# The first layer norm moved into the scan, chunk by chunk, with identity products in TensorE's waits

## The chip, the core and the metric

The kernel runs on one core of a Trainium2 chip. Its time is device time in microseconds (us), from the first to the last instruction of one execution. Before the change three runs took 568.33, 569.10 and 570.53 us; the median is 569.1.

The engines are named as the profile does: PE is TensorE's matmul, PEld its weight load, DVE is VectorE, ACT ScalarE, POOL GpSimd, SP SyncE. A "q" behind the name (SPq, ACTq) is the engine's sequencer, which issues DMAs and waits.

## What is computed

Two blocks with a residual each, on `x` of shape 4 x 1024 x 128:

```python
h = _layernorm(x, axis=-1) * (1 + ca) + sa
x = x + ga * _L0_attn_ref(h, W_Q, W_KV, W1, b1, W2, b2)
h = _layernorm(x, axis=-1) * (1 + cb) + sb
x = x + gb * _L0_ffn_ref(h, ...)           # 8 experts, 2 chosen per token, and a shared one
```

The first block is a scan over the 1024 time steps. At each step the four batches' `k_t` and `v_t` (from `kv = h @ W_KV`) give one step of gradient descent on a small MLP, and the MLP as it stands at the end maps `q = h @ W_Q`:

```python
def step(params, kvt):
    k_t, v_t = kvt
    g = jax.grad(loss_fn)(params, k_t, v_t)     # loss: mean((silu(k W1 + b1) W2 + b2 - v)^2)
    return tuple((p - LR * gp for p, gp in zip(params, g))), None
params, _ = jax.lax.scan(step, (W1, b1, W2, b2), (k, v))
```

`sa`, `ca`, `ga`, `sb`, `cb`, `gb` are six rows per batch, `silu(c) @ wmod`.

## The kernel before

**Stages.** Four blocks of code follow each other. Each block has one stream of instructions per engine, and a barrier of all five engines ends it: the next block begins when the last engine, SP included, has come to the end of its stream.

1. *Prologue* (lines 188 to 408). `x` is loaded to `xr` in quarters `s_x[0..3]` (SP, 16 DMAs of 128 KB), the weights by ACT's queue. DVE takes `bn_stats` of all 32 chunks and computes mean and reciprocal root in two halves (`spread`, 16 small steps each). POOL normalises the first 12 chunks, DVE the other 20, into `hstage`; PE turns them (32 transposes); ACT applies scale and shift per batch (`modulate`) and writes `hT`, the transposed `h` of all chunks.
2. *Scan* (lines 410 to 1274). The 1024 steps are cut into 32 chunks (`CH`) of 32 steps x 4 batches = 128 columns. Within a chunk the recurrence is solved by repeated passes over 128 x 128 matrices. The steps have names: `q_...` prepare a chunk (`q_proj`: k and v from `hT`; `q_copy` to `kv`; `q_turn`, `q_rows`, `q_shift`: their transposes; `q_gram`, `q_mask`: the masked products `GX`; `q_low`: a bf16 copy `GXb`). `l_...` are the passes in bf16, `h_...` the passes in fp32 on the same chunk one turn later, `x_...` an extra pass for chunk 0, `c_...` a check of how far the last pass moved. In the names `act` is silu, `tan` its tanh, `less` is a - 1, `slope` the derivative, `tq`/`rq` a transpose and its copy back, `y` the forecast, `e` its error, `f` the error sent back, `g` the gradient, `z` the preactivation, `W1`/`W2`/`b1`/`b2` the updates.
3. *The step-by-step scan* is skipped where the check holds, as it does here.
4. *Tail* (from line 1276): `q` through the MLP, second layer norm, routing, experts, output.

**What sets the order in the scan.** `turn(n, r)` is a list written out by hand per engine: `do(step, n + k, r + k)` places the step of chunk n + k in turn n. It runs for n = -3 to 32: turns -3 to 3 straight, turns 4 to 27 in a loop of 6 x 4 turns (`Fori(1, CH // RING - 1)`), turns 28 to 32 straight. An engine works through its list in order, each step waiting for the semaphores of its inputs, so a step that waits holds up all that stand behind it on its engine.

The lines that the prediction speaks of most, all on PE in this list: `l_f1` (line 494, `bank<-W2pL,e2L`), `l_y4` (`bank<-aL,W2pL` behind `l_te`), `h_zp` (`bank<-GXb,gL` behind `l_y4`), `h_tq0` (line 607, `bank<-ident,qH`), `l_te4` (line 572). Almost all matmuls bear line 494, that of the helper `mm`.

Of the kernel before, what the change touches and what calls it, by code (L numbers as in the profile page):

```python
# [60 lines left out]
def program(nc, x, w_q, w_kv, w1, b1, w2, b2, w_router,  # L61
            s_w1t, s_b1, s_w2t, s_b2, cond, w_mod, slabs, ident_in, before_in, lower_in, tabs_in, xs, ys, out):
    with ExitStack() as ctx:
# [122 lines left out]
        POOL_NORMS = 3  # L186
        with ExitStack() as stack, block() as blk:  # L187
            psb = phase(stack)
            difq, nrq, epsq = (psb(n, [P, CH]) for n in ("difq", "nrq", "epsq"))
# [61 lines left out]
            def _(act):
# [34 lines left out]
                for g in range(NG):  # L286
                    modulate(g)
# [1931 lines left out]
```

## Time and profile before

| | |
|---|---|
| median of 3 runs | 569.1 us |
| profiled execution | 572.98 us, its span 571.2 us |
| prologue | 0 to 35.8 us |
| scan | 35.8 to about 294 us |
| tail | from 294.6 us |
| busy in the span | PE 90%, DVE 71%, ACT 65%, POOL 56% |

Times in the profile count from the span's start and come from the one profiled execution; 1.8 us of its time lie outside the span. A row of the timeline gives start, duration, engine, line, operation, `output<-inputs`, shapes, count, and in brackets how long the engine had been idle before and what ended that. Rows of PE overlap, since matmuls are pipelined: what a step takes of PE's time is read from one start to the next. The granted clock (PEclk) is a share of TensorE's full 2.4 GHz; 0.50 is 1.2 GHz. The trace has no record of it before 55 us and prints 1.00 there.

### The profile page before, as it was taken

How to read it: one execution, taken by the hardware profiler on the slowest of the kernel's cores; microseconds unless marked ns; L12 is line 12 of the kernel's file. 1: busy time of each engine (PE TensorE's matmuls, PEld its weight loads, DVE VectorE, ACT ScalarE, POOL GpSimd, SP SyncE). 2: the span in 40 equal slices, each digit the busy share in tenths (PEclk: the TensorE clock that was granted, in tenths of full speed). 3: DMA queues.
4: the chain of work that ended last, by engine and by line, in shares of the span. 5: the costliest groups of instructions: out<-in, count | busy, mean ns of one | idle time of the engine just before them, and what ended most of it. 6: DMA issues, size and time to landing. Idle time of an engine off the chain costs nothing. (4 is left out here: it accounts for less than half of the span.)

```text
span 571.2 us, 13378 instructions
## 1 busy us (share of the span) xinstructions
PE 512.1 (90%) x4049; PEld 462.3 (81%) x4049; DVE 405.2 (71%) x1620; ACT 369.6 (65%) x1325; POOL 319.3 (56%) x451
## 2 busy tenths in 40 slices
PE   3277999999999999999977878989899999999992
PEld 2255999999999999999744868979799999999992
DVE  2745888888888888888838788845934555555766
ACT  2365999999999999998835738844344444444440
POOL 2602444444444444444425188888888888766761
PEclk9999999999999999999979598999999999999997
DMA  9249990000000000000000011645546678778936
GB/s 195 29 157 402 393 372 7 2 0 0 0 0 0 0 0 0 0 0 2 2 2 0 2 47 45 211 122 155 147 127 182 195 244 242 226 224 281 350 123 193
DMA packets 39795, 66.75 MB, mean 117 GB/s; under 512 B 7522, under 2 KB 26724, under 8 KB 39748
## 3 DMA queue, kind: packets, MB, share of 16 engines
q1 hardware_dynamic: 31220, 54.45, 30.5%
q0 software_dynamic: 4544, 9.45, 4.7%
q10 hardware_dynamic: 3984, 2.30, 1.6%
q8 instruction: 21, 0.34, 0.2%
q14 instruction: 26, 0.21, 0.1%
HBM read 36.26 MB, written 29.92 MB: 116 GB/s over the span
## 5 line engine op out<-in xcount | busy, mean ns | idle before, releaser
L1666 ACT ACTIVATE hid<-bank,slab 128x256 f32<-128x256 f32 x156 | 64.0, 470 | 84.5 <-PE bank L1526 84.4
L2129 POOL DMA_INDIRECT ys<-yo,dst x78 | 76.3, 979 | 33.0 <-DVE yo L2006 16.5
L2121 POOL DMA_INDIRECT xs<-hrow,slot_i x64 | 63.0, 984 | 35.8 <-issue 35.3
L1540 PEld LDWEIGHTS bank<-slab,hid 128*128 128x128 f32 x624 | 77.0, 194 | 2.2
L1526 PE MATMUL bank<-hg,slab 128*128 128x256 f32 x312 | 74.6, 383 | 2.8 <-issue 2.2
L1540 PE MATMUL bank<-slab,hid 128*128 128x128 f32 x624 | 77.0, 277 | 0.0
L1526 PEld LDWEIGHTS bank<-hg,slab 128*128 128x128 f32 x312 | 56.6, 191 | 9.5 <-issue 3.3
L2001 DVE TENSOR_TENSOR yb<-bank,slab 128x256 f32<-128x256 f32 x39 | 16.6, 425 | 61.4 <-PE bank L1540 61.1
L1235 POOL TENSOR_TENSOR diff<-ge 128x256 f32<-128x256 f32 x32 | 23.2, 725 | 45.6 <-DVE ge L986 45.6
L1251 POOL TENSOR_TENSOR nH<-aH,ones 128x128 f32<-128x128 f32 x32 | 14.6, 455 | 38.6 <-ACT aH L897 38.6
L986 DVE SCALAR_TENSOR_TENSOR gL<-qrowL,bank 128x128 bf16<-128x128 bf16 x65 | 18.7, 288 | 19.1 <-PE bank L494 15.3
L2104 POOL MEMSET rested<- 128x1408 f32 x25 | 32.2, 1290 | 0.0
L2006 DVE TENSOR_SCALAR yo<-yb,gt 128x128 f32<-128x128 f32 x78 | 30.4, 532 | 1.4
L1247 POOL TENSOR_TENSOR GXb<-GX,ones 128x256 bf16<-128x256 f32 x32 | 23.2, 726 | 13.5 <-DVE GX L986 13.5
L1243 POOL TENSOR_TENSOR nL<-aL,ones 128x128 f32<-128x128 bf16 x32 | 13.7, 429 | 26.1 <-ACT aL L867 26.1
L494 PE MATMUL bank<-GX,ge 128*128 128x128 f32 (+1 forms) x128 | 28.1, 302 | 0.0
L1239 POOL TENSOR_TENSOR nH<-aH,ones 128x128 f32<-128x128 f32 x32 | 14.6, 455 | 22.4 <-ACT aH L851 22.4
L494 PE MATMUL bank<-kv 128*128 128x128 f32 x128 | 22.8, 304 | 1.0 <-ACT kv L827 1.0
L494 PE MATMUL bank<-hT,wkv 128*128 (+1 forms) x128 | 21.3, 292 | 2.0 <-PEq L187 1.9
L494 PE MATMUL bank<-GXb,gL 128*128 128x128 bf16 x97 | 22.3, 230 | 0.7 <-DVE gL L986 0.7
L494 PE MATMUL bank<-aL,W2pL 128*128 128x128 bf16 x97 | 21.5, 222 | 1.2 <-DVE GaL L986 0.8
L1499 PE MATMUL bank<-sw,hs 128*128 128x128 f32 x144 | 21.4, 302 | 1.3 <-ACT hs L1656 1.3
(381 smaller groups left out, 1784.7 us busy)
## 6 DMA issues: line engine op xcount, KB each, us to landing
slab<-in_slabs_dram SPq DMA_DIRECT2D x39, 578.0 KB, 4.1
xs<-fill SPq DMA_DIRECT2D x34, 528.0 KB, 7.4
xt<-xs SPq DMA_DIRECT2D x39, 132.0 KB
yg<-ys SPq DMA_DIRECT2D x7, 512.0 KB, 5.7
xr<-in_L_attn_x_dram SPq DMA_DIRECT2D x16, 128.0 KB, 7.1
ys<-yo,dst POOLq DMA_INDIRECT x78, 3.4
out_dram<-xr SPq DMA_DIRECT2D x18, 64.0 KB, 2.0
xs<-hrow,slot_i POOLq DMA_INDIRECT x64, 2.3
```

The costliest lines, as they stand in the source:

```text
L494: return pe.matmul(dst, lhs, rhs, start=start, stop=stop, skip_group_check=True)
L986: return dve.scalar_tensor_tensor(out=dst, in0=a, scalar=s, in1=b, op0=o0, op1=o1)
L1235: pool.tensor_tensor(diff[r % 2][:, :, :], ge[r % 2][1][:, :, :], ge[r % 2][0][:, :, :], ALU.subtract).then_inc(diff_made, 1)
L1247: pool.tensor_tensor(GXb[r][:, :, :], GX[r][:, :, 0:P], ones2[:, :].rearrange("p (k t) -> p k t", k=2), ALU.mult).then_inc(GXb_made, 1)
L1499: mm = pe.matmul(y[:, s * D:(s + 1) * D], hs[t % 2][:, n, s * P:(s + 1) * P], sw[:, 1, n, :], start=(n == 0), stop=(n == FT - 1), skip_gro ...
L1526: mm = pe.matmul(e_half(i, n), left[:, n * P:(n + 1) * P], right, start=True, stop=True)
L1540: mm = pe.matmul(y[:, s * D:(s + 1) * D], hid[i % 2][:, n, s * P:(s + 1) * P], right, start=(n == 0), stop=(n == FT - 1), skip_group_check ...
L1666: nc.scalar.activation(hid[i % 2][:, n, :], e_half(i, n), ACT.Gelu_apprx_tanh, bias=bias).then_inc(e_x, 1)
L2006: dve.tensor_scalar(yo[v][:, s, :], yb[i % 2][:, s, :], gt[v][:, s:s + 1], None, ALU.mult).then_inc(e_yo, 1)
L2104: nc.gpsimd.memset(rested[:, :], 0.0).then_inc(pause_done, 1)
L2121: pool.indirect_dma_start(out=xs[:, :], out_offset=bass.IndirectOffsetOnAxis(ap=slot_i[:, i, c:c + 1], axis=0), in_=hrow[:, c, :], in_offs ...
L2129: pool.indirect_dma_start(out=ys[:, :], out_offset=bass.IndirectOffsetOnAxis(ap=dst[v][:, s:s + 1], axis=0), in_=yo[v][:, s, :], in_offset ...
```

## The change

1. **Prologue cut short.** Only the first quarter of `x` (chunks 0 to 7) gets its statistics there. The `hstage` passes, the transposes and `modulate` are gone. SP loads the first quarter, then small tensors that ACT's queue had loaded, waits for `wmod`, and only then loads the other three quarters and the rest. PE makes rows of `sa` and `1 + ca` (`sarow`, `carow`) and multiplies the identity by itself four times.
2. **Layer norm inside the scan.** New steps per chunk: POOL `n_0` (normalise), `n_1` (times `carow`), `n_2` (plus `sarow`); PE `n_t` (transpose); ACT `n_c` (copy to `hT`). DVE begins the scan with the 24 remaining `bn_stats`, and computes the other 24 chunks' mean and root in pieces `f_0` to `f_11` between the steps of the first turns; likewise the gates (`g_0` to `g_4`).
3. **No loop**: all 36 turns are written out.
4. **Another order** of the steps in every engine's list, another layout of PSUM banks, `q_...` one chunk ahead rather than two or three.
5. **Identity products on PE**: 12 at the scan's start, 4 behind every step as long as n < 0, and 6 in fp32 behind the scan's last product.

```diff
@@ prologue, SP @@
-                for q in range(4):
-                    ...
-                sp.dma_start(tabs[:, :], tabs_in).then_inc(s_b, 16)
+                load(0)
+                sp.dma_start(tabs[:, :], tabs_in).then_inc(s_tabs, 16)
+                for dst, src in ((wkv[:, :], w_kv), (W1[:, :], w1), (before[:, :], before_in),
+                                 (b1c[:, :], ...), (b2c[:, :], ...), (wq[:, :], w_q)):
+                    sp.dma_start(dst, src).then_inc(s_small, 16)
+                sp.wait_ge(s_mod, 16)
+                for q in range(1, 4):
+                    load(q)
                 sp.dma_start(mkh[:, :], lower_in).then_inc(s_b, 16)
                 ...
-                sp.wait_ge(s_b, 16 * 6)
+                sp.wait_ge(s_tabs, 16)
@@ scan, PE @@
+                filling = [True]
+
+                def do(step, c, r):
+                    if not isinstance(c, int) or 0 <= c < CH:
+                        step(c, r % RING)
+                        if filling[0]:
+                            for i in range(4):
+                                mm(bank[1][:, 0:P], identb[:, :], identb[:, :], True, True)
+                def n_t(c, r):
+                    pe.wait_ge(hs2_made, c + 1)
                     after(pe, GX_made, c)
+                    pe.transpose(NT, hrows[r % 2][:, :], ident[:, :]).then_inc(NT_made, 1)
-                for n in range(-3, RING):
-                    turn(n, n % RING)
-                with pe.Fori(1, CH // RING - 1) as ring:
-                    for r in range(RING):
-                        turn(ring * RING + r, r)
-                for n in range(CH - RING, CH + 1):
+                for i in range(12):
+                    mm(bank[1][:, 0:P], identb[:, :], identb[:, :], True, True)
+                for n in range(-3, CH + 1):
+                    filling[0] = n < 0
                     turn(n, n % RING)
                 ...
                 pe.drain().then_inc(scan_left, 1)
+                for i in range(6):
+                    mm(bank[1][:, 0:P], ident[:, :], ident[:, :], True, True)
                 pe.wait_ge(holds_step, 4)
@@ scan, ACT @@
+                def n_c(c, r):
+                    act.wait_ge(NT_made, c + 1)
+                    nc.scalar.copy(hT[:, c, :], NT).then_inc(hT_made, 1)
@@ scan, DVE @@
+                def f_1(c, r):
+                    settle(2)
+                    both_of(mean[:, late], difq[:, late], -0.5, me, ALU.mult, ALU.add)
+                    both_of(tmp[:, late], difq[:, late], 0.25, difq[:, late], ALU.mult, ALU.mult)
+                    both_of(var[:, late], var[:, late], 1.0 / D, epsq[:, late], ALU.mult, ALU.add)
+                for q in range(1, 4):
+                    dve.wait_ge(s_x[q], 16 * B)
+                    for c in range(q * QUARTER, (q + 1) * QUARTER):
+                        dve.bn_stats(stats[:, c, :], xr[:, c, :]).then_inc(bn_ready, 1)
@@ scan, POOL @@
+                def n_2(c, r):
+                    pool.wait_ge(hs1_made, c + 1)
+                    pool.tensor_tensor(hrows[r % 2][:, :], hscaled[r % 2][:, :], sarow[:, :], ALU.add).then_inc(hs2_made, 1)
+                def n_0(c, r):
+                    at_chunk(pool, c, 5, rstd_ready, 2)
+                    pool.tensor_scalar(hplain[r % 2][:, :], xr[:, c, :], mean[:, c:c + 1], rstd[:, c:c + 1], ALU.subtract, ALU.mult).then_inc(hs0_made, 1)
+                def n_1(c, r):
+                    pool.wait_ge(hs0_made, c + 1)
+                    pool.tensor_tensor(hscaled[r % 2][:, :], hplain[r % 2][:, :], carow[:, :], ALU.mult).then_inc(hs1_made, 1)
```

**PE, second half of a turn.** Numbers behind a name are the buffer. Before, from `l_y4` (the two rows into bank3) by way of `h_zp` (`GXb3,gL11`) to `l_te4` (line 572):

```order
L494 MATMUL bank3<-aL11,W2pL0 128x128 [waits erowL1_made]
L494 MATMUL bank3<-GaL11,erowL11 128x128
L494 MATMUL bank1<-GXb3,gL11 128x128 [waits gL1_made]
L494 MATMUL bank6<-erowL11,arowL1 128x128
L494 MATMUL bank6<-arowL1,erowL11 128x129
L494 MATMUL bank7<-kv1,kv0 128x128 [waits kv_made]
L494 MATMUL bank7<-kv1 128x128
L572 MATMUL bank4<-identb,eX1 128x128 [waits eX_made]
L494 MATMUL bank3<-eX1 128x128
L494 MATMUL bank0<-kv0,W1b 128x129 [waits W1n_made]
L494 MATMUL bank0<-GXb0,gL11 128x128 [waits GXb_made]
```

The same place in the changed kernel:

```order
L433 MATMUL bank3<-aL11,W2pL0 128x128 [waits erowL1_made]
L433 MATMUL bank3<-GaL11,erowL11 128x128
L433 MATMUL bank5<-ge01,arowH0 128x128
L433 MATMUL bank5<-arowH0,ge01 128x129
L433 MATMUL bank1<-GXb3,gL11 128x128 [waits b1x_made]
L433 MATMUL bank6<-erowL11,arowL1 128x128
L433 MATMUL bank6<-arowL1,erowL11 128x129
L433 MATMUL bank4<-eX1 128x128 [waits eX_made]
L603 MATMUL bank3<-identb,eX1 128x128
L608 MATMUL bank2<-ident,hrows1 128x128 [waits GX_made,hs2_made]
L433 MATMUL bank0<-kv0,W1b 128x129 [waits W1n_made]
```

`h_s2` (the two fp32 products into bank5) now stands ahead of `h_zp`, where nothing stood; `q_gram` (bank7 before) has left this place for one ahead of `l_te`; `n_t` (line 608) is new.

**POOL, one turn.** Before:

```order
L1239 TENSOR_TENSOR nH00<-aH00,ones2 128x128 [waits aH0_made]
L1243 TENSOR_TENSOR nL10<-aL10,ones2 128x128 [waits aL0_made]
L1247 TENSOR_TENSOR GXb2<-GX2,ones2 128x256 [waits GX_made]
L1251 TENSOR_TENSOR nH01<-aH01,ones2 128x128 [waits aH1_made]
L1226 TENSOR_TENSOR vb0<-kvrow2,tabs 128x128 [waits kvrow_made]
L1230 TENSOR_TENSOR nL11<-aL11,ones2 128x128 [waits aL1_made]
L1235 TENSOR_TENSOR diff0<-ge01,ge00 128x256 [waits G_made,E_made]
```

Now:

```order
L1318 TENSOR_TENSOR nH00<-aH00,ones2 128x128 [waits aH0_made]
L1322 TENSOR_TENSOR nL10<-aL10,ones2 128x128 [waits aL0_made]
L1326 TENSOR_SCALAR hplain1<-xr,mean,rstd 128x128
L1330 TENSOR_TENSOR hscaled1<-hplain1,carow 128x128 [waits hs0_made]
L1289 TENSOR_TENSOR nH01<-aH01,ones2 128x128 [waits aH1_made]
L1297 TENSOR_TENSOR nL11<-aL11,ones2 128x128 [waits aL1_made]
L1301 TENSOR_TENSOR hrows1<-hscaled1,sarow 128x128 [waits hs1_made]
L1306 TENSOR_TENSOR diff0<-ge01,ge00 128x256 [waits E_made,G_made]
L1310 TENSOR_TENSOR GXb2<-GX2,ones2 128x256 [waits GX_made]
L1314 TENSOR_TENSOR vb0<-kvrow2,tabs 128x128 [waits kvrow_made]
```

`n_0` and `n_1` (lines 1326, 1330) stand where the copy `GXb` stood, ahead of `h_less1` (`nH01`); the copy and `vb` now come at the end of the turn, ahead of the next `h_less0`.

**PE, the scan's start.** The changed kernel's first rows. `identb` against itself (line 433, bank1) are the identity products:

```order
L433 MATMUL bank1<-identb 128x128 x12
L608 MATMUL bank2<-ident,hrows0 128x128 [waits hs2_made]
L433 MATMUL bank1<-identb 128x128 x4
L433 MATMUL bank2<-hT,wkv 128x128 [waits hT_made]
L433 MATMUL bank2<-hT,wkv 128x128
L433 MATMUL bank1<-identb 128x128 x4
L519 MATMUL bank4<-ident,kv0 128x128 [waits kv_made]
L520 MATMUL bank4<-ident,kv0 128x128
```

Before, the scan began with the products of `hT` and `wkv` at once, since `hT` was finished for all chunks; now `n_t` of chunk 0 and its three steps on POOL stand ahead.

## Rows read from the trace of the kernel before

**Rows 1.** Busy us and (count) by stretch: PE, PEld, DVE, ACT, POOL, PEclk, DMA, GB/s

```profile
58.50:284.50 226.00, 225.00 (x2208) 206.93 (x2206) 195.22 (x848) 206.60 (x910) 106.57 (x210) 1.00 0.12 47
```

**Rows 2.** One line's instructions: PE's L572 (`l_te4`), one per turn

```profile
L572 PE MATMUL bank<-identb,eX x32: 219/219/314, 53.8 to 284.5; 128*128 128x128 bf16 x32
```

**Rows 3.** The tile xr: SP's issues, ns min/median/max, first and last start

```profile
L206 SPq DMA_DIRECT2D xr<-in_L_attn_x_dram x16: 378/452/1134, 0.7 to 9.6; - x16
```

**Rows 4.** Timeline of the prologue: the last issue of SP's queue

```profile
14.70 0.70 SPq L213 DMA_DIRECT2D bs2row<-in_L_ffn_bs_dram  x2
```

**Rows 5.** Timeline of the prologue, DVE and POOL

```profile
7.55 1.65 DVE L325 BATCH_NORM_STATS2 stats<-xr 128x6 f32<-128x128 f32 x8 [7.55 <-DMA xr<-in_L_attn_x_dram]
13.55 0.19 DVE L336 SCALAR_TENSOR_TENSOR difq<-stats 128x16 f32<-128x16 f32 x1
16.10 0.17 DVE L336 SCALAR_TENSOR_TENSOR rstd<-tmp,difq 128x16 f32<-128x16 f32 x1
...
16.44 9.40 POOL L222 TENSOR_SCALAR hstage<-xr,mean,rstd 128x128 f32<-128x128 f32 x12 [12.81 <-DVEq L367]
```

**Rows 6.** Timeline of the scan's fill, PE, then DVE, then POOL

```profile
35.85 1.19 PE L494 MATMUL bank<-hT,wkv 128*128 128x128 f32 x4 [1.87 <-PEq L187]
37.53 1.23 PE L494 MATMUL bank<-kv 128*128 128x128 f32 x4 [0.49 <-ACT kv L827]
...
42.40 0.31 PE L494 MATMUL bank<-GXb,gL 128*128 128x128 bf16 x1
...
38.79 0.43 DVE L986 SCALAR_TENSOR_TENSOR GX<-bank,mk 128x256 f32<-128x256 f32 x1 [3.68 <-PE bank L494]
...
39.30 0.72 POOL L1247 TENSOR_TENSOR GXb<-GX,ones 128x256 bf16<-128x256 f32 x1 [13.46 <-DVE GX L986]
```

**Rows 7.** Timeline of PE: `l_ga1` of chunk 0 and of chunk 1

```profile
49.91 0.31 PE L494 MATMUL bank<-aL 128*128 128x128 bf16 x1
...
58.52 0.22 PE L494 MATMUL bank<-aL 128*128 128x128 bf16 x1
```

**Rows 8.** PE in one turn: `l_f1`, `h_s2`, `l_te`, `l_y4`, `h_zp`, `h_tq0`, `l_f1`

```profile
153.69 0.23 PE L494 MATMUL bank<-W2pL,e2L 128*128 128x128 bf16 x1
...
156.28 0.45 PE L494 MATMUL bank<-ge,arowH 128*128 128x128 f32 x2
...
156.79 0.22 PE L538 MATMUL bank<-identb,eL 128*128 128x128 bf16 x1
...
157.46 0.22 PE L494 MATMUL bank<-aL,W2pL 128*128 128x128 bf16 x1
...
157.57 0.23 PE L494 MATMUL bank<-GXb,gL 128*128 128x128 bf16 x1
...
159.58 0.32 PE L607 MATMUL bank<-ident,qH 128*128 128x128 f32 x1
...
161.09 0.23 PE L494 MATMUL bank<-W2pL,e2L 128*128 128x128 bf16 x1
```

**Rows 9.** Timeline of the same turn: `h_act0`, `h_less0`, `h_slope0`

```profile
157.84 0.37 ACT L851 ACTIVATE aH<-bank,bp 128x128 f32<-128x128 f32 x1
...
158.28 0.46 POOL L1239 TENSOR_TENSOR nH<-aH,ones 128x128 f32<-128x128 f32 x1 [0.61 <-ACT aH L851]
...
159.23 0.28 DVE L986 SCALAR_TENSOR_TENSOR qH<-bank,nH 128x128 f32<-128x128 f32 x1
```

**Rows 10.** Timeline of PE: `l_te4` of the last two chunks

```profile
277.13 0.23 PE L572 MATMUL bank<-identb,eX 128*128 128x128 bf16 x1 [0.27 <-DVE eX L986]
...
284.49 0.23 PE L572 MATMUL bank<-identb,eX 128*128 128x128 bf16 x1 [0.27 <-DVE eX L986]
```

**Rows 11.** Timeline of PE at the tail's start

```profile
296.62 3.62 PE L1424 MATMUL bank<-hT,wz 128*128 128x512 f32 x4
...
302.16 5.69 PE L1424 MATMUL bank<-hT,wz 128*128 128x512 f32 x12
```

**Rows 12.** A stretch of the tail's start, columns as in rows 1

```profile
298.00:300.00 2.00, 2.00 (x3) 0.62 (x2) 0.00 (x0) 0.69 (x1) 2.00 (x3) 0.50 0.00 0
```

More of the change, by code:

```diff
@@ L283, in _ @@
[L283 to L287 removed]
+                nc.scalar.copy(sarow[:, :], bank[4][:, 0:D])
+                nc.scalar.activation(carow[:, :], bank[4][:, D:2 * D], ACT.Identity, bias=ones[:, 0:1])
+                act.wait_ge(mod_ready, 2)
+                nc.scalar.copy(sbrow[:, :], bank[5][:, 0:D])
@@ L310, in _ @@
-                for i, n in enumerate((3, 4)):
-                    pe.matmul(bank[4][:, i * D:(i + 1) * D], lhs, wmod[:, n * D:(n + 1) * D], start=True, stop=True)
-                pe.wait_ge(s_small, 128)
-                pe.transpose(bank[2][:, 2 * P:3 * P], W2[:, :], ident[:, :])
-                pe.transpose(bank[2][:, 3 * P:4 * P], wq[:, :], ident[:, :]).then_inc(mod_ready, 1)
-                for g in range(NG):
-                    turn(g)
+                pe.wait_ge(s_small, 16 * 6)
+                pe.transpose(bank[2][:, 0:P], wq[:, :], ident[:, :]).then_inc(mod_ready, 1)
@@ L318, in _ @@
+                for i in range(4):
+                    pe.matmul(bank[1][:, 0:P], ident[:, :], ident[:, :], start=True, stop=True)
             @blk.vector
@@ L381, in _, with settle, both_of @@
-                statistics(3)
-                spread(1)
-                for g in range(POOL_NORMS, NG):
-                    normalise(g)
-                dve.wait_ge(s_small, 128)
+                me, mo = stats[:, soon, 1], stats[:, soon, 4]
+                def settle(n):
+                    taken[0] += n
+                    dve.wait_ge(ln_rstd_step, taken[0])
+                def both_of(out, in0, scalar, in1, op0, op1):
+                    dve.scalar_tensor_tensor(out=out, in0=in0, scalar=scalar, in1=in1, op0=op0, op1=op1).then_inc(ln_rstd_step, 1)
@@ L1264, in turn @@
-                    do(h_less1, n, r)
-                    do_first(x_less, n + 1, r + 1)
-                for n in range(-3, RING):
-                    turn(n, n % RING)
-                with pool.Fori(1, CH // RING - 1) as ring:
-                    for r in range(RING):
-                        turn(ring * RING + r, r)
-                for n in range(CH - RING, CH + 1):
+                    do(n_0, n + 3, r + 3)
+                    do(n_1, n + 3, r + 3)
+                for n in range(-3, CH + 1):
```

1024 lines of the change are left out of this document (523 added, 501 removed).

## Prediction

> **What bounds the kernel now.** I read the busy shares by stretch first, then the timelines of the prologue, the fill and one turn, and last the seam between scan and tail. Three stretches differ in what ends last.
>
> In the prologue every engine waits for something: `x` lands, DVE takes statistics, POOL and DVE normalise, PE turns, ACT modulates all 32 chunks, and PE's first product of the scan starts at 35.85 [rows 6]. None of that work is needed beyond chunk 0 for the scan to begin.
>
> In the scan PE is busy for 225.00 of 226.00 us [rows 1]. That doesn't make it PE's throughput alone. A turn takes 161.09 - 153.69 = 7.40 us [rows 8]; at the end, where no chunk is left to prepare and PE has some 1.1 us less to do per turn (four fp32 products at about 0.22 to 0.25 each and two transposes, by the 0.51 of `h_s2`'s two from 156.28 to 156.79 [rows 8]), `l_te4` still comes 284.49 - 277.13 = 7.36 us after the one before [rows 10]. So the dependency from chunk to chunk is about as long as PE's work, and the order decides how they interlock.
>
> At the seam PE has idled, and the clock granted is 0.50 [rows 12]: four matmuls of line 1424 take 3.62 us, the next twelve 5.69 [rows 11].
>
> The sum is made against the profiled execution (572.98, span 571.2). The median run is 3.9 below it; I take the same difference off both.
>
> **Prologue: -18.9.** DVE's part would end at: first eight statistics 7.55 + 1.65 = 9.20; the sixteen small steps 16.27 - 13.55 = 2.72 [rows 5]; eight small copies, an estimate of 1.1: 13.0. But the barrier waits for SP too, and that is late next. SP issues an `xr` DMA in 0.45 (median), up to 1.13 when the queue is full; the sixteen run from 0.75 to 9.6 + 1.13 = 10.8, so 0.63 each [rows 3]. The rest of its list ends at 15.40 [rows 4], 4.6 later; less 0.5 for `tabs`, that is 4.1 for what still stands last. Now: four loads and seven small ones at 0.49 end at 6.1; `wmod` should have landed; twelve loads at 0.49 to 0.63 are 5.9 to 7.6; plus 4.1: SP ends between 16.1 and 17.8. I take 16.7 and 0.2 for the barrier: the scan starts at 16.9 instead of 35.8. Bounds: 15.5 (SP never held up) and 18.0.
>
> **Fill: +1.6.** Before, from the first product to `l_zx` of chunk 0 (42.40, `bank<-GXb,gL`): 6.55 us [rows 6]. Now, ahead of that product: `n_0` at 9.40/12 = 0.78 [rows 5], `n_1` and `n_2` at 0.46 as `h_less0` [rows 9], each with a wait of 0.1; then `n_t` and `n_c`, about 0.8 by the 1.68 from 35.85 to 37.53 that twice the work and its copy need [rows 6]. That is 2.7. `kv` follows after 1.7, then `q_turn` and identity products ahead of `q_gram` (0.9 at the slow pace), 1.26 to `GX` (37.53 to 38.79), 0.5 and 0.72 to `GXb` [rows 6]: 7.8; if PE is still slow, `n_t`, `l_zb` and twelve identity products hold `l_zx` until 8.5. I take 8.2, so +1.6 (bounds +1.2, +2.2). DVE's 24 statistics, 24 x 0.206 = 4.9 us, lie beside this, since `q_mask` first needs DVE at about +6.5. Eight more microseconds of loading lie beside it too. The second chunk's preparation, which stood in the old fill, is gone from this path and makes up part.
>
> **First passes: about 0.** From `l_zx` to `l_ga1` of chunk 0 took 7.51 us, and the turn after it 8.61 against 7.40 later [rows 6 to 8]. The same product lasts 0.31 there and 0.23 in the turn [rows 6, 8]: PE ran at half pace. The identity products may bring full pace earlier (8 or so hops at 0.08: -0.6) but stand ahead of steps that wait (about five groups of four, 0.2 to 0.4 each, partly in waits), and the pieces `f_` stand between DVE's steps of the extra pass. I take +0.1, bounds -1.5 and +1.5.
>
> **Thirty turns: +2.0.** `n_t` adds 0.11 to 0.15 to PE. ACT and POOL have room: 206.60 and 106.57 of 226 busy [rows 1], `n_c` 0.27, the POOL steps 1.7 of 7.4. Following PE's new order from `l_f1`:
> - `l_f1` to `l_y4`: 3.77 before [rows 8]. `h_s2` leaves, `q_gram` comes, `q_proj` now stands in the wait for `l_g0`: 3.70.
> - `l_y4` to `h_zp`: 0.11 before. Now `h_s2` stands between, 0.51: 0.62.
> - `h_zp` to `h_tq0`: 2.01 before. The chain in it is `h_act0` 0.27 after `h_zp`, `h_less0` 0.44 later, 0.46 for it, 0.14, `h_slope0` 0.28, 0.06 [rows 8, 9]: 1.65. Before, DVE came to `h_slope0` late (159.23, while POOL ended at 158.74) and PE had 2.0 us of work. Now PE's work there is 1.5, so the chain shows: 1.68.
> - `h_tq0` to the next `l_f1`: 1.51 before, same steps: 1.52.
>
> Sum 7.52; with rounding I take 7.50. The old turns average (284.5 - 53.8)/31 = 7.44 [rows 2]; without the slower first one 7.43, 0.03 over the 7.40 of [rows 8], which I put down to the loop's branches. So +0.07 x 30 = +2.1. Bounds: 7.30 (just below the 7.36 without preparation; an order could shorten the chain) and 7.84 (`h_s2` in full, no chain given back): -3.9 to +12.3. The written-out turns cost nothing that I can see: the old straight turns at 58.52 on had the same period while the stores to `xs` kept the DMA engines full. The Trainium skill ("Runtime: NRT & Kernel Launch", Instruction fetch mechanics) says that straight code is fetched ahead and that a taken branch can stall; by it the loop's end is a gain of under 1 us, which I have counted.
>
> **Seam: -1.5.** The six fp32 identity products run while DVE makes `holds`. If they keep the clock up, the four matmuls cost 4 x 0.474 = 1.9 instead of 3.62, and some 0.9 goes at the smaller ones ahead: 2.6, of which POOL's and DVE's work hides part. The Trainium skill ("TensorE: Matmul & The Clock Gate", Part 1) says that the clock follows how busy PE has been lately and that the moment of the switch is not tied to the kernel's start. By it the gain would be the whole 2.6 in some executions and none in others. I take -1.5.
>
> **Sum.** -18.9 + 1.6 + 0.1 + 2.0 - 1.5 = -16.7. Profiled 556.3; median 569.1 - 16.7 = **552.4 us**. Its own range: 547 to 558.
>
> **Rivals.**
> 1. *The turn grows more.* `h_s2`'s half microsecond stays on the chain because `h_less0` comes late: POOL's `c_diff`, `GXb` and `vb` (0.72 + 0.72 + 0.46) now stand right ahead of it, behind `n_2`. For it: before, POOL idled only 0.61 ahead of `h_less0` [rows 9]. Against: by my walk `vb` ends 0.2 before `h_act0` does. With turns of 7.7 to 7.84: 552.4 + 6 to 10 = 558 to 563.
> 2. *The turn shrinks.* The new order hides the waits, turns of 7.30 to 7.4, SP at 15.5, the seam's gain whole: 552.4 - 3 to 6 for the turns, - 1.4, - 1.1: 541 to 547. For it: PE's 225 of 226 us contain some 0.9 us per turn that is neither of its products (30 bf16 at 0.056, by the two from 157.46 to 157.57, 18 fp32 at 0.22 and 7 transposes at half that make 6.4 to 6.5; an estimate by the pace of [rows 8]). Against: the 7.36 of rows 10.
> 3. *Slower than before.* POOL's three new steps, 1.7 us, enter the chain: `n_0` and `n_1` (1.3 us) stand ahead of `h_less1`, the rest ahead of `h_less0`, and whatever exceeds POOL's idle time is paid in every turn. It decides from 16.7 + 2.0 = 18.7 over 30 turns: 0.62 us per turn, a turn of 8.05. If all 1.7 counted: 552.4 + 45 = 598. Against: POOL's idle time is 119 us in 226 [rows 1], 3.9 per turn.
> 4. *The prologue isn't shortened as said.* `wmod` or the later quarters land late, since the small weights now share SP's queue with them, SP or DVE's statistics wait, and the scan's first mask comes after 28: about 557 to 560.
>
> **Chances.** Forecast 0.62; rival 1 0.14; rival 2 0.15; rival 3 0.03; rival 4 0.06. Range with all bounds, leaving out the far ends of rivals 1, 2 and 3: **545 to 560**. A measurement of this kernel tells 0.5% (2.8 us) from no change; only rival 3 and a corner of rival 1 reach that: faster 0.95, same 0.02, slower 0.03.
>
> **What would show it.** The scan's first product at 16 to 18, and SP the last at the barrier. `l_zx` of chunk 0 about 8.2 later. `l_ga1` of chunk 1 near 41.5 (now 58.52). `n_t` 7.5 us apart in the steady part, with PE waiting a tenth or two ahead of `h_tq0` and POOL's idle time ahead of `h_less0` gone. Line 1424's counterpart at full pace from its first matmul. A period of 7.7 or more makes the turn's term wrong; a scan start at 14 or at 20, the SP term; a first mask that waits for DVE's statistics, the term of the fill.

## The result and the profile after

The changed kernel took 557.15 us (median of 6 runs, 554.89 to 558.66); the kernel before, on the same chip, 570.47 (568.33 to 572.16). The ratio is 0.9759, 95% interval 0.9738 to 0.9779: 13.3 us less. The forecast was 552.4 with a range of 545 to 560.

| | before | after |
|---|---|---|
| profiled execution, its span | 572.98, 571.2 us | 554.89, 553.1 us |
| scan's first product | 35.85 | 15.61 |
| `l_ga1` of chunk 1 | 58.52 | 40.58 |
| `l_te4` of chunk 1, of chunk 31 | 61.56, 284.49 | 44.02, 270.23 |
| the tail's first twelve matmuls (L1497, before L1424) | 302.16 | 287.19 |
| from there to the end | 269.0 | 265.9 |

The profiled execution of after was the fastest of its six, and that of before (572.98) took longer than any of its six: 4.8 us of the 18.1 between the two are that choice. The part of the program that the change touches ends with the seam, and there the gain is 302.16 - 287.19 = 15.0 us.

Busy time of 30 turns in the changed kernel answers to [rows 1] (columns: stretch, its length, PE, PEld, DVE, ACT, POOL busy with counts, PEclk, DMA, GB/s):

```profile
40.60:266.60 226.00, 222.89 (x2212) 205.85 (x2211) 201.37 (x841) 200.55 (x927) 154.34 (x295) 1.00 0.12 44
```

POOL has 154.34 where it had 106.57; PE is as full as it was. The timeline of the changed kernel at the barrier answers to [rows 3 to 5]:

```profile
5.99 5.85 SPq L202 DMA_DIRECT2D xr<-in_L_attn_x_dram  x12
...
12.76 0.22 DVE L347 TENSOR_SCALAR mk<-before 128x128 f32<-128x128 f32 x1
12.86 1.18 SPq L216 DMA_DIRECT2D sb<-in_L_ffn_bs_dram  x1
14.08 0.97 SPq L218 DMA_DIRECT2D bs2row<-in_L_ffn_bs_dram  x2
...
15.61 0.81 PE L433 MATMUL bank<-identb 128*128 128x128 bf16 x8 [2.72 <-PEq L192]
...
15.61 0.68 DVE L1229 BATCH_NORM_STATS2 stats<-xr 128x6 f32<-128x128 f32 x3 [2.63 <-PEq L192]
```

SP issues until 15.05, while DVE was done at 12.98 and idles 2.63 us: SP was last, as forecast. The twelve loads took 5.85 us, 0.49 each, the forecast's lower bound. The fill, against [rows 6] and [rows 7]:

```profile
15.71 0.80 POOL L1326 TENSOR_SCALAR hplain<-xr,mean,rstd 128x128 f32<-128x128 f32 x1 [12.07 <-POOLq L192]
...
22.34 0.43 DVE L954 SCALAR_TENSOR_TENSOR GX<-bank,mk 128x256 f32<-128x256 f32 x1 [1.87 <-PE bank L433]
...
23.78 0.22 PE L433 MATMUL bank<-GXb,gL 128*128 128x128 bf16 x1
...
31.55 0.31 PE L433 MATMUL bank<-aL 128*128 128x128 bf16 x1
...
40.58 0.22 PE L433 MATMUL bank<-aL 128*128 128x128 bf16 x1
```

`l_zx` of chunk 0 comes 23.78 - 15.61 = 8.17 us after the scan's start (forecast 8.2), and DVE, its statistics done, waits 1.87 us for the first mask. One turn of the changed kernel answers to [rows 8]:

```profile
152.56 0.22 PE L433 MATMUL bank<-W2pL,e2L 128*128 128x128 bf16 x1
...
156.30 0.22 PE L433 MATMUL bank<-aL,W2pL 128*128 128x128 bf16 x1
...
156.91 0.22 PE L433 MATMUL bank<-GXb,gL 128*128 128x128 bf16 x1
...
158.52 0.32 PE L641 MATMUL bank<-ident,qH 128*128 128x128 f32 x1
...
160.07 0.22 PE L433 MATMUL bank<-W2pL,e2L 128*128 128x128 bf16 x1
```

The four pieces are 3.74, 0.61, 1.61 and 1.55 us, 7.51 in all; the forecast had 3.70, 0.62, 1.68, 1.52. The chain inside the third, against [rows 9]:

```profile
157.17 0.37 ACT L867 ACTIVATE aH<-bank,bp 128x128 f32<-128x128 f32 x1
...
157.61 0.45 POOL L1318 TENSOR_TENSOR nH<-aH,ones 128x128 f32<-128x128 f32 x1 [0.18 <-ACT aH L867]
...
158.17 0.29 DVE L954 SCALAR_TENSOR_TENSOR qH<-bank,nH 128x128 f32<-128x128 f32 x1
```

DVE now takes `h_slope0` as soon as POOL's `nH` is there (158.06); in [rows 9] it came half a microsecond late. PE is hardly held up at `h_tq0` itself (some 0.02 us); its pause in this stretch, 0.24 us, lies earlier, ahead of the product of `GaL` and `erowX` at 157.84. The seam against [rows 11] (a product in fp32 counts twice in these rows, so x12 are the six identity products):

```profile
276.69 0.28 PE L433 MATMUL bank<-ones,ge 128*128 128x1 f32 x2
277.07 1.60 PE L433 MATMUL bank<-ident 128*128 128x128 f32 x12
278.60 0.19 PE L747 MATMUL bank<-holds,ones 128*1 128x4 f32 x2
280.82 0.46 PE L1617 MATMUL bank<-W1b,wqT 128*128 128x128 f32 x2 [2.02 <-PEq L349]
...
281.95 3.47 PE L1497 MATMUL bank<-hT,wz 128*128 128x512 f32 x4
...
287.19 5.69 PE L1497 MATMUL bank<-hT,wz 128*128 128x512 f32 x12
```

The four matmuls of L1497 are hardly faster than before (3.47 against 3.62): the clock was still full up to 280.8 and then fell, as the second of these stretches shows against [rows 12]:

```profile
277.00:280.80 3.80, 1.72 (x14) 1.51 (x15) 1.16 (x9) 0.40 (x4) 0.02 (x1) 1.00 0.00 0
282.50:285.20 2.70, 2.70 (x4) 0.95 (x3) 0.14 (x1) 0.69 (x1) 2.68 (x3) 0.50 0.04 9
```

### The profile page after: what moved, and what is told of

The parts are those of the page before. It is cut to its first block and busy times, and to the rows that moved or that the text cites. A ratio compares the mean times of both kernels' runs of the same rounds, so it can differ in the third digit from the quotient of the medians.

```text
span 553.1 us, 13467 instructions
## 1 busy us (share of the span) xinstructions
PE 506.3 (92%) x4129; PEld 460.5 (83%) x4129; DVE 408.4 (74%) x1600; ACT 355.2 (64%) x1325; POOL 365.1 (66%) x535
## 5 line engine op out<-in xcount | busy, mean ns | idle before, releaser
L1613 PEld LDWEIGHTS bank<-slab,hid 128*128 128x128 f32 x624 | 75.8, 192 | 2.0
L2079 DVE TENSOR_SCALAR yo<-yb,gt 128x128 f32<-128x128 f32 x78 | 35.9, 604 | 1.4
L1326 POOL TENSOR_SCALAR hplain<-xr,mean,rstd 128x128 f32<-128x128 f32 x32 | 25.4, 793 | 12.1 <-POOLq L192 12.1
L954 DVE SCALAR_TENSOR_TENSOR qH<-bank,nH 128x128 f32<-128x128 f32 x64 | 18.7, 292 | 19.3 <-POOL nH L1289 18.9
L1289 POOL TENSOR_TENSOR nH<-aH,ones 128x128 f32<-128x128 f32 x32 | 14.6, 457 | 26.8 <-ACT aH L780 26.8
L2041 DVE COPY hg<-bank 128x256 f32<-128x256 f32 x39 | 23.7, 607 | 0.3 <-PE bank L1581 0.2
L896 ACT COPY ge<-bank 128x128 f32<-128x128 f32 x32 | 8.5, 266 | 22.3 <-PE bank L433 22.3
L1572 PEld LDWEIGHTS bank<-sw,hs 128*128 128x128 f32 x144 | 19.6, 206 | 2.8 <-issue 1.1
```

The source lines that it names most:

```text
L1326: pool.tensor_scalar(hplain[r % 2][:, :], xr[:, c, :], mean[:, c:c + 1], rstd[:, c:c + 1], ALU.subtract, ALU.mult).then_inc(hs0_made, 1)
L1572: mm = pe.matmul(y[:, s * D:(s + 1) * D], hs[t % 2][:, n, s * P:(s + 1) * P], sw[:, 1, n, :], start=(n == 0), stop=(n == FT - 1), skip_gro ...
L1613: mm = pe.matmul(y[:, s * D:(s + 1) * D], hid[i % 2][:, n, s * P:(s + 1) * P], right, start=(n == 0), stop=(n == FT - 1), skip_group_check ...
L2041: dve.tensor_copy(hg[j % 2][:, :], fed(j)).then_inc(e_hg, 1)
L2079: dve.tensor_scalar(yo[v][:, s, :], yb[i % 2][:, s, :], gt[v][:, s:s + 1], None, ALU.mult).then_inc(e_yo, 1)
```

## The experiments

"Marks" below are places on PE's timeline of each profiled execution: the usual turn is `l_te4` to `l_te4`; 30 turns run from chunk 1 to chunk 31; the seam from the product of `ones` and `ge` to the tail's twelve matmuls; the rest from there to the end. `l_te4` is line 603 in the changed kernel. Where the second column says "one execution", there is no other; e7 goes through the step-by-step scan behind turn 32, so that its seam and rest say nothing here.

| kernel | ratio to before (95%) | `l_te4` chunk 1 | usual turn | 30 turns | seam | rest |
|---|---|---|---|---|---|---|
| before | 1 | 61.56 | 7.407 | 222.93 | 11.52 | 269.0 |
| after | 0.9759 (0.9738, 0.9779) | 44.02 | 7.516 | 226.21 | 10.50 | 265.9 |
| c0_again | 0.9754 (0.9721, 0.9787) | 43.52 | 7.516 | 226.20 | 10.61 | 272.3 |
| e1_no_fill_products | 0.9754 (0.9731, 0.9777) | 43.91 | 7.516 | 226.18 | 10.50 | 271.9 |
| e2_no_seam_products | 0.9782 (0.9756, 0.9808) | 44.46 | 7.516 | 226.21 | 10.82 | 273.1 |
| e3_small_loads_later | 0.9708 (0.9683, 0.9734) | 40.55 | 7.516 | 226.22 | 10.59 | 273.3 |
| e4_zp_ahead | 0.983 (0.9798, 0.9863) | 43.01 | 7.712 | 231.71 | 10.42 | 267.6 |
| e5_before_written_out | 1.0 (0.9972, 1.0029) | 61.27 | 7.402 | 222.73 | 11.48 | 271.1 |
| e7_no_norm_steps | one execution | 43.03 | 7.516 | 226.12 | | |
| e8_n0_twice | one execution | 43.88 | 7.549 | 227.04 | 12.01 | 264.3 |
| e9_dve_op_two_places | one execution | 43.19 | 7.93, 7.52 | 232.14 | 10.63 | 267.6 |
| e10_less_in_the_row | 0.9724 (0.9693, 0.9755) | 40.56 | 7.579 | 227.38 | 8.38 | 270.2 |
| e11_gram_earlier | 0.9883 (0.984, 0.9925) | 41.46 | 7.915 | 237.13 | 8.38 | 270.5 |
| e12_best | 0.9645 (0.9614, 0.9677) | 39.93 | 7.516 | 225.73 | 8.38 | 266.4 |

**c0_again: the changed kernel once more.**

> The changed kernel once more, unaltered. Theory A: what the two profiled executions differ in behind the scan (the experts' part began 17.65 us earlier, though the scan's last chunk was only 14.3 earlier) is scatter of that one execution; then the scan's marks repeat to 0.1 us (first product 15.6, l_te4 of the last chunk 270.2, apart from single stalls of 0.3 to 0.4 us), while the stretch from the tail's first twelve matmuls of line 1497 to the end, 265.9 us, comes out elsewhere within 265 to 270; the median lies at 557 within 1 us. Theory B: the tail is shorter because of the change (its DMAs or code meet it in another phase); then the stretch repeats as 265.9 to 266.5 and the clocks' records look alike.

Theory A in kind: the rest took 272.3 us instead of 265.9, so the 265.9 were scatter, and more of it than the 265 to 270 expected. The scan's marks repeat within 0.5 us (0.1 was expected) and the usual turn is 7.516 again. Over the table, unchanged code of the tail takes 264 to 273. The median was 561.08 against 575.63 on a slower chip: the absolute time missed theory A's 557, the ratio repeated.

**e1: no identity products in the fill.**

```diff
-                for i in range(12):
-                    mm(bank[1][:, 0:P], identb[:, :], identb[:, :], True, True)
-                    filling[0] = n < 0
+                    filling[0] = False
```

> Identity products of the fill left out (the 12 at the scan's start and the groups of 4 for n < 0). Theory A (as in the prediction: they bring full pace earlier and cost about as much where they stand ahead of a step): l_ga1 of chunk 1, now at 40.6, comes at 40.0 to 41.5 and the time is within 1 us of the changed kernel. Rival B (they are what wins the clock): PE stays at half pace through turns 0 and 1, l_ga1 of chunk 1 at 42.5 or later, time +2 to +4 us. Rival C (they only stand in the way): l_ga1 of chunk 1 at 39.5 or before, time -1 us or more.

Theory A. The scan's start is at 15.61 in both; without the products `l_zx` comes at 23.10 instead of 23.78, and `l_ga1` of chunk 0 at 31.48 instead of 31.55: the 0.7 us that they cost in the fill they give back in the first passes. Without them the granted clock is 0.50 from 16 to 36 us (0.29 to 0.31 a product); with them it is 1.00 from 22.7 to 29.5. `l_ga1` of chunk 1 comes at 40.47 and 40.58. Medians 561.05 and, in c0_again, 561.08.

**e2: no identity products at the seam.**

```diff
-                for i in range(6):
-                    mm(bank[1][:, 0:P], ident[:, :], ident[:, :], True, True)
                 pe.wait_ge(holds_step, 4)
```

> The six fp32 identity products behind the scan's last product left out, nothing else. Theory A (they keep part of the clock at the seam, worth about 1 us: ones x ge to the twelve matmuls of line 1497 took 11.5 us before and 10.5 after): 11.3 to 11.6 us without them, time +0.8 to +1 us. Rival B (the clock's fall comes by its own phase and the products do nothing): 10.4 to 10.6 us, time unchanged. Rival C (they cost: the product of holds stands behind them): 10.3 or less, time -0.2 us.

Between A and B: the seam is 0.2 to 0.3 us longer. (The median, 563.19 against 561.08 in c0_again, rose by 2.1 us, within the scatter of the executions, 558.4 to 564.4.) What rival C named is true as well. Without them the product of `holds` runs 1.35 us after that of `ones` and the tail starts after 3.56; with them, 1.91 and 4.13:

```profile
277.13 0.28 PE L433 MATMUL bank<-ones,ge 128*128 128x1 f32 x2
278.48 0.19 PE L745 MATMUL bank<-holds,ones 128*1 128x4 f32 x2 [1.07 <-DVE holds L1239]
280.69 0.77 PE L1615 MATMUL bank<-W1b,wqT 128*128 128x128 f32 x2 [2.02 <-PEq L349]
```

The products stand ahead of a product that everyone waits for, cost 0.57 us there and, by these two traces, bring 0.8 to 0.9 behind it. So most of the seam's 1.0 us between before and after isn't their merit. How little these tenths are worth shows e8, which has the products as well: there the clock fell at 281.8 and stayed at 0.50 until 288.6 (in the changed kernel until 285.5), and the seam took 12.01 us, longer than without the products and longer than before. Six other executions with them took 10.42 to 10.63.

**e3: SP's small loads behind the barrier.** SP's first entries of the scan's block instead of its last of the prologue's:

```diff
@@ prologue, SP; the same five loads then stand first in the scan's SP @@
-                sp.dma_start(mkh[:, :], lower_in).then_inc(s_b, 16)
-                ...
                 sp.wait_ge(s_tabs, 16)
```

> SP issues mkh, wrT, sb1 and bs2row (five DMAs, 3.2 us) at the start of the scan's block instead of the end of the prologue's. Theory A (SP ended last at the barrier, DVE is next at 13.0): the scan's first product comes at 13.2 to 13.5 instead of 15.6, and the time falls by 2.0 to 2.4 us. Rival B (something else of the scan's start depends on what lands late, DVE's statistics of the late quarters for one): the first product comes earlier but l_zx of chunk 0 stays within 0.5 us of 23.8, no gain. Rival C (the barrier waits for DMAs or for POOL): first product at 15 or later.

Theory A, and more: the scan starts at 13.28 instead of 15.6 to 15.8, `l_te4` of chunk 1 comes 3.0 us before that of c0_again, the time falls by 2.5 (558.62 against 561.08 on the same chip).

```profile
13.24 0.35 SPq L403 DMA_DIRECT2D mkh<-in_lower_dram  x1
...
13.28 0.83 PE L433 MATMUL bank<-identb 128*128 128x128 bf16 x12 [0.70 <-PEq L192]
...
13.28 3.19 DVE L1229 BATCH_NORM_STATS2 stats<-xr 128x6 f32<-128x128 f32 x16 [0.30 <-PEq L192]
```

DVE idles 0.30 us at the barrier instead of 2.63: it is last now.

**e4: `h_zp` ahead of `h_s2`.**

```diff
-                    do(h_s2, n - 1, r - 1)
                     do(h_zp, n, r)
+                    do(h_s2, n - 1, r - 1)
```

> PE's h_zp put ahead of h_s2's four matmuls, all else as in the changed kernel. The turn is 7.516 us now. Theory A (the chain h_zp, h_act0, h_less0, h_slope0, h_tq0 takes part in setting the turn, as the prediction's walk has it; h_zp can go 0.34 us earlier, when DVE's bp is written, but POOL is in vb until 0.14 us before h_less0 starts now): turns of 7.38 to 7.45, scan 2 to 4 us shorter. Rival B (PE's own work sets the turn, the walk only happened to fit): 7.50 to 7.52. Rival C (POOL doesn't hold it up): 7.2. Rival D (h_s2's results, which now come 0.1 us later, are waited for): 7.55 or more.

All but D fail: the turn is 0.196 longer. DVE's timeline says where:

```profile
157.65 0.22 DVE L954 SCALAR_TENSOR_TENSOR bp<-bank,bp 128x1 f32<-128x1 f32 x2
157.98 0.35 DVE L954 SCALAR_TENSOR_TENSOR eX<-bank,b2L,kv 128x128 bf16<-128x128 f32 x1
158.25 0.28 DVE L954 SCALAR_TENSOR_TENSOR W1b<-bank,W1b 128x128 f32<-128x128 f32 x1
158.70 0.43 DVE L954 SCALAR_TENSOR_TENSOR W2p<-bank,W2q 128x257 f32<-128x257 f32 x1 [0.17 <-PE bank L433]
```

`h_zp` stands on PE until `bp` is written, and `h_s2` behind it is late; DVE's `h_W2` (`W2p`) waits 0.17 us for it, and all of DVE's list with it. In the changed kernel there is no wait at this place.

**e7: the norm's steps left out.**

```diff
@@ n_t, n_0, n_1, n_2 alike; n_c waits for min(c + 1, 4) @@
+                    if c >= 4:
+                        return
```

> Left out: n_0, n_1, n_2 (POOL) and n_t (PE) for chunks 4 to 31; ACT's n_c stays and copies chunk 3's h again, so the output isn't the reference's. Theory A (n_t costs PE its own 0.11 us and the POOL steps cost nothing, lying in its idle time): turns of 7.38 to 7.42, which is the old 7.41. Rival B (the three POOL steps are on the chain as well): 7.2 or less. Rival C (the turn is set by a chain that none of them is on): 7.50 to 7.52.

Rival C: 7.516. Neither PE's transpose nor POOL's 1.7 us cost a turn anything. (With the norm gone the passes don't settle, the step-by-step scan runs too and the whole takes 9.4 ms; the other instructions of the passes are the same.)

**e8: `n_0` twice.**

```diff
+                    pool.tensor_scalar(spare[r % 2][:, :], xr[:, c, :], ..., ALU.subtract, ALU.mult).then_inc(extra_made, 1)
                     pool.tensor_scalar(hplain[r % 2][:, :], xr[:, c, :], ..., ALU.subtract, ALU.mult).then_inc(hs0_made, 1)
```

> POOL does n_0 twice per turn (the first into a spare tile): 0.80 us more ahead of h_less1, where it idles 0.67 us now. This measures the third rival of the prediction. Theory A (only what exceeds the idle time is paid, and h_less1 is on the chain): turns of 7.60 to 7.75. Rival B (h_less1 has slack of its own behind it): 7.52. Rival C (POOL slows DVE while both work): 7.52 plus 0.3 or more from DVE's rows growing.

7.549, between A and B: POOL no longer idles ahead of `h_less1`, and the 0.8 us more cost 0.033 per turn. So POOL had some 0.7 us of room per turn there. Rival C doesn't show. (The seam of 12.01 in the table is the clock's, as said at e2; the edit doesn't touch it.)

**e9: one DVE operation more, in two places.**

```diff
+                    dve.tensor_tensor(spare[r % 2][:, :], ident[:, :], ident[:, :], ALU.mult).then_inc(extra_made, 1)
@@ turn, DVE: for odd chunks ahead of c_acc, for even ones ahead of h_slope1 @@
```

> DVE does one product of 128x128 f32 more per turn (0.2 us start to start), into a spare tile: for odd chunks ahead of c_acc, in the stretch in which DVE never waits; for even chunks ahead of h_slope1, where DVE idles 0.59 us per turn. Turns are 7.516 now. Theory A (formed from e7 and e4: DVE's unbroken row from h_slope1 to h_g0, 5.6 us, and the way from h_g0 by ACT, PE and POOL back to h_slope1, 1.96 us, set the turn, PE's own products don't): turns alternate, 7.70 to 7.72 and 7.51 to 7.53, the scan about 3 us longer. Rival B (PE sets the turn): 7.52 in both. Rival C (the chain by h_less0 alone sets it and DVE is at its limit nowhere): 7.52 to 7.6 in both.

Theory A in kind: turns alternate. In DVE's idle time 0.2 us cost nothing (7.52), in the unbroken row 0.41, twice what was expected. Timeline of DVE and POOL in such a turn:

```profile
159.33 0.28 DVE L1104 TENSOR_TENSOR spare<-ident 128x128 f32<-128x128 f32 x1
...
159.49 0.46 POOL L1334 TENSOR_TENSOR nH<-aH,ones 128x128 f32<-128x128 f32 x1 [0.20 <-ACT aH L869]
159.53 0.43 DVE L1116 TENSOR_TENSOR sums<-sums,acc 128x4 f32<-128x4 f32 x1
```

`sums` (128x4, 0.15 us in all the turns between) takes 0.43 and ends at 159.96, when POOL's `nH` does (159.95); so it is in each of the longer turns of the thirty, to 0.02 us. Pushed by 0.2 us it starts 0.04 us behind a POOL operation and, by this, is held until that one ends. The other way round nothing is held: in the next turn the added product starts at 162.89, ahead of a POOL product at 163.01, and takes its usual 0.28. The Trainium skill ("GPSIMD Engine Reference", 8. Key points) says that GpSimd shares its SBUF interfaces with VectorE and that DVE instructions with two SBUF inputs contend; the trace agrees, 0.28 us for this one.

**e10: less in DVE's row, and the seam's products behind that of `holds`.**

```diff
@@ to e3; turn, DVE @@
+                    do(c_acc, n - 2, r - 2)
                     do(h_slope1, n - 1, r - 1)
                     ...
-                    do(c_acc, n - 1, r - 1)
                     do(l_me, n, r)
                     do(l_W2, n, r)
-                    do(l_b2, n, r)
                     ...
                     do(l_e1, n + 1, r + 1)
+                    do(l_b2, n, r)
                     do(l_ma0, n + 1, r + 1)
@@ scan's end, PE: the loop of six products stands behind this @@
                 pe.matmul(bank[0][0:1, 0:4], ones[:, 0:1], holds[:, :], ...).then_inc(total_ready, 1)
```

> e3 and two edits more. DVE: c_acc (0.07 us) goes from the unbroken row into the idle time ahead of h_slope1, l_b2 (0.06) behind h_e2 and l_e1, where DVE waits for PE. PE: the six fp32 identity products go behind the product of holds instead of ahead of it. Theory A (DVE's row sets the turn): turns of 7.38 to 7.46 instead of 7.516, 30 of them 1.7 to 4 us shorter. Rival B (h_less0's chain is within 0.05 of it and takes over): 7.46 to 7.50. Rival C (no effect): 7.516. At the seam: ones x ge to the tail's first product 3.6 instead of 4.1 us, and line 1497 still at its faster start, so 9.9 to 10.1 to its twelve matmuls against 10.6; rival: 10.6, since the clock falls earlier.

The turn got longer, 7.579, which none of the theories had. `h_slope0` starts 1.03 us after `l_te4` as before (1.04): POOL's `nH` sets it, and the 0.13 us freed ahead of it are waited away. Behind it DVE never waits, and `l_b2`'s 0.06 there are paid in full; e12, where `l_b2` alone is back in its place, confirms it. At the seam:

```profile
274.40 0.28 PE L433 MATMUL bank<-ones,ge 128*128 128x1 f32 x2
275.74 0.19 PE L745 MATMUL bank<-holds,ones 128*1 128x4 f32 x2 [1.07 <-DVE holds L1242]
275.87 1.61 PE L433 MATMUL bank<-ident 128*128 128x128 f32 x12
277.96 0.46 PE L1618 MATMUL bank<-W1b,wqT 128*128 128x128 f32 x2 [0.49 <-PEq L344]
...
279.09 1.88 PE L1498 MATMUL bank<-hT,wz 128*128 128x512 f32 x4
...
282.78 5.69 PE L1498 MATMUL bank<-hT,wz 128*128 128x512 f32 x12
```

8.38 us instead of 10.5, more than expected: the products run in the barrier's wait, delay nobody, and the clock stays full through the tail's start (1.88 for the four matmuls).

**e11: `q_gram` earlier.** On PE `do(q_gram, n + 1, r + 1)` put ahead of `do(h_te3, n - 1, r - 1)`, to e10.

> e10, and on PE q_gram ahead of h_te3: DVE's GX, which waits 0.1 us for q_gram inside its row, can begin 0.1 earlier; h_te3's result has 0.3 us of slack by the trace. Theory A (each wait inside DVE's row is paid in full): turns 0.07 to 0.11 shorter than e10's. Rival B: unchanged, because l_te or h_W2's wait for h_s2 takes over. Rival C (h_te3 is on the chain): longer by 0.1 or more.

Rival C: 0.34 longer. ACT waits for `h_te3`, and with it `qrowL` behind, for which DVE's `gL` waits:

```profile
158.41 0.27 ACT L840 COPY ge<-bank 128x128 f32<-128x128 f32 x1 [0.38 <-PE bank L548]
...
158.87 0.26 ACT L848 COPY qrowL<-bank 128x128 bf16<-128x128 bf16 x1
...
159.23 0.29 DVE L954 SCALAR_TENSOR_TENSOR gL<-qrowL,bank 128x128 bf16<-128x128 bf16 x1 [0.51 <-ACT qrowL L848]
```

The 0.3 us of slack that I read from `h_te3`'s own consumer was none, since an engine's list stands still behind it.

**e5: the kernel before with its loop written out.** `Fori` over 6 x 4 turns replaced by a Python loop on the four engines.

> The kernel before with one edit: the loop of 6 x 4 turns written out. Before, l_te4 came every 7.407 us, but the six loop ends cost 0.07 each, its entry 0.24 and its exit 0.27 with what follows. Theory A (prediction: the branches are all that a loop costs, and written-out code costs nothing): thirty turns in 222.93 less 0.9 = 222.0 to 222.2. Theory B (written-out code has stalls of its own on DVE, as the changed kernel shows two, 0.37 and 0.31 us, at the same turns in each execution): no gain, 222.6 to 223.2. In both the time is within 0.3% of before.

Theory B, by the turns: the usual one falls to 7.402 and the loop's extras go, but two turns take 7.76 and one 7.53; 30 turns gain 0.2 us. Only one of the two is DVE's own (0.36 us at one instruction with nothing late); in the other DVE waits 0.36 us longer for PE. The ratio is 1.000.

**e12: what the runs bear out.** e3, the seam of e10, and `c_acc` alone moved.

> The three edits that the runs so far bear out or leave open: SP's small loads at the scan's start (e3), the six identity products behind the product of holds (e10), and DVE's c_acc alone moved into the idle time ahead of h_slope1 (l_b2 back in its old place). Theory A (in e10 it was l_b2, standing ahead of GaL, that made the turn 0.063 longer, and c_acc only frees time that h_less0's chain takes at once): turns of 7.50 to 7.52. Rival B (c_acc in the idle time costs, since it holds up h_slope1): 7.54 to 7.58. Rival C (DVE's row binds after all): 7.44 to 7.47. Seam as in e10, 8.3 to 8.5 us from ones x ge to the twelve matmuls, against 10.5. The two single stalls of the thirty turns may vanish as in e10, 0.7 us. Together against the changed kernel: -2.4 and -2.1, and -0.7 or nothing: 4.5 to 5.2 us less, a ratio to before of 0.966 to 0.968; its thirty turns 225.4 to 226.3.

Theory A: 7.516. The single stalls shrink to one of 0.21 and one of 0.04. The median is 549.16 against 568.79: ratio 0.9645, 19.6 us less than before and about 6 less than the changed kernel, more than forecast. Some 1.5 us of it no edit aimed at: `l_ga1` of chunk 0 comes 14.4 us after the scan's start instead of 15.9, and the clock was full through the fill (columns as above, first e12_best, then the changed kernel):

```profile
16.00:24.00 8.00, 6.05 (x71) 4.89 (x70) 5.03 (x27) 2.71 (x10) 3.54 (x7) 1.00 0.99 354
```

```profile
16.00:24.00 8.00, 6.91 (x50) 5.68 (x49) 4.90 (x25) 1.86 (x4) 4.23 (x8) 0.58 0.92 348
```

An earlier start alone doesn't bring it. e10 has the same full clock and the same 14.4 us, but e3 and e11, which start as early (13.28 and 13.47, against 13.57 in e10 and 13.00 in e12), ran a part of the fill at half pace (the four products of `hT` and `wkv` in 1.22 us instead of 0.71) and took 15.2 and 15.7. What decides it stays open.

## Why the prediction was right, and where it wasn't

- *Prologue, -18.9: -20.2.* SP was last, as said, and e3 shows it by taking its last loads away. The size missed by 1.3: SP's list ended at 15.05 and not at 16.7, since the twelve loads took 0.49 each and `sb1` 1.18 instead of 2.09 us; the barrier took 0.56 and not 0.2. The scan began at 15.61, beside the bound of 15.5. (The prediction put the longer issues before, up to 1.13 us, down to a full queue; no run shows that.)
- *Fill, +1.6: +1.6.* 8.17 us to `l_zx`; the statistics lay beside it.
- *First passes, about 0: +1.1.* `l_zx` to `l_ga1` of chunk 0 took 7.77 (before 7.51), the turn behind it 9.03 (8.61), and from there to `l_te4` of chunk 1 3.44 (3.04). Half pace isn't the reason: PE ran at it from 29.5 to 36.3, but before through the whole of this passage (0.29 to 0.31 a product from 42.4 to 54.7), and e1 bears out the 0.6 us that the prediction hoped to win: without the identity products the first piece takes 8.38. So the passes themselves are slower, by 0.9 in that piece, where DVE has the pieces `f_`, which the prediction named without a price. Behind it the gates' pieces `g_` (`gtm`, `gate`) stand ahead of steps that PE waits for:

```profile
39.17 0.41 DVE L954 SCALAR_TENSOR_TENSOR gtm<-gate 128x256 f32<-128x256 f32 x1
39.50 0.28 DVE L954 SCALAR_TENSOR_TENSOR gL<-qrowL,bank 128x128 bf16<-128x128 bf16 x1
...
40.77 0.49 DVE L954 SCALAR_TENSOR_TENSOR gate<-gtm 128x256 f32<-128x256 f32 x1
41.19 0.28 DVE L954 SCALAR_TENSOR_TENSOR GaL<-bank,mk 128x128 bf16<-128x128 f32 x1
```

  Set beside the trace of before, PE falls behind by 0.37 us up to the product that needs this `gL`, and by another 0.30 up to the one that needs this `GaL`. The prediction didn't price the `g_` pieces at all; with them this is the term that missed most in kind. That they cause it is read from the traces; no run takes them out.
- *Thirty turns, +2.0: +3.3.* The walk gave 7.52 and the turn is 7.516; rounding it to 7.50 cost 0.5 us. The agreement is in part luck: the four pieces miss by 0.04, 0.01, 0.07 and 0.03 and cancel. The other 0.7 are two turns of 7.89 and 7.83, the same in after, c0_again, e1, e2, e3 and e7: DVE stands still at one instruction (0.35 and 0.22 us) while nothing that it waits for is late.

```profile
52.46 0.15 DVE L954 SCALAR_TENSOR_TENSOR b2L<-bank,W2p 128x1 f32<-128x1 f32 x1
52.95 0.29 DVE L954 SCALAR_TENSOR_TENSOR qH<-bank,nH 128x128 f32<-128x128 f32 x1 [0.35 <-issue]
```

  The prediction said that written-out turns cost nothing; this and e5 say otherwise. The Trainium skill ("Runtime: NRT & Kernel Launch", Instruction fetch mechanics), which the prediction followed for the loop's end, says that a taken branch can stall and that straight code is fetched ahead. On the branches e5 agrees: the 0.07 us at each loop end are gone when the loop is written out. On straight code no run here decides, since it was not shown that the stalls are fetches.
- *What the walk rested on.* Its sum held, its grounds in part. It counted PE's work and one chain; e7 shows that `n_t` costs nothing, so PE's own work doesn't set the turn. What does, as I read it from the traces with e4 and e8 to e12, is an interlock: the chain `h_zp`, `h_act0`, `h_less0`, `h_slope0` that the prediction named, from there the stretch of DVE's list up to `h_g0` in which it never waits, the way back by ACT, PE and POOL to `h_slope1` (in which DVE idles 0.59 us), and again DVE without a wait. Each change of order that I made inside it left the turn as it was or made it longer, so no run has shown it by a shorter turn. Nor does any take back the change's parts one by one: which of the new order, the other banks and the preparation one chunk ahead made 7.516 of 7.407 stays open.
- *Seam, -1.5: -1.0.* And for the wrong reason: e2 gives the identity products 0.2 to 0.3 of it, and e8 takes even that back. The clock fell all the same, only later, in each kernel that has them ahead of the product of `holds`: the prediction had the gain as whole or nothing, and whole it was never. Some 0.4 lie in DVE's end of the scan, whose first `holds` starts 0.94 us behind the product of `ones` (in after and in e2) instead of 1.32. The rest is the time at which the clock fell and rose.
- *Sum, -16.7: -15.0* at the tail's twelve matmuls. The terms missed by -1.3, 0, +1.0, +1.3 and +0.5, and 0.3 us more lie between the last `l_te4` and the seam, where the prediction has no term. That the first miss makes up for one of the others is luck. Behind the seam lies only code that the change leaves alone, and its time scatters over 9 us. Of the 4.8 us between 552.4 and 557.15, 1.7 are this sum's, 1.4 the kernel before's, 570.47 beside these runs and not 569.1, and 1.7 are left: the marks say 15.0, the 95% interval of the medians 12.6 to 14.9, that of c0_again 12.3 to 16.1. Whether that is scatter or a small loss behind the seam stays open.
- *Rivals.* Rival 1: at 7.516 the turn didn't grow more; POOL idles 0.18 us ahead of `h_less0`. Rival 3: by e7 POOL's three steps cost a turn nothing, where 0.62 us would have made a loss. Rival 2's SP at 15.5 came true, its turns of 7.3 did not. Nothing of `wmod` or the late quarters was waited for (rival 4). Two sums in them are wrong: rival 2's terms give 544 to 547, not 541, and 1.7 us in 30 turns are 51, not 45. Neither touches the forecast.
- *Signs.* Two that the prediction named failed: the tail's first four matmuls of line 1497 ran at half pace, and ahead of `h_tq0` PE hardly waits (0.02 us). The scan's start at 15.61 and `l_ga1` of chunk 1 at 40.58 came a little before the 16 to 18 and the 41.5 named.

## What to carry to other kernels

Follow each engine's list to its idle time before pricing an operation: the same 0.2 us cost nothing in DVE's idle slot and 0.41 in its unbroken row, and two of PE's steps swapped cost 0.2 or 0.34 per turn because of what stood behind them on another engine. When a prologue is cut, the sequencer with the longest list of small loads is the next to end it; move loads that nobody needs yet past the barrier (2.5 us here). Here the products that keep TensorE's clock up did their work behind the last product that others wait for (2.1 us) and little or nothing ahead of it.
